# Attention's key and query loads issued by GpSimd, negated-maxima rows first in the sync engine's order, and a lead of 8 blocks in place of 12

## The reference

```python
x = x + attn(layernorm(x))      # 16 heads of 16; the part that the change touches
x = x + ffn(layernorm(x))       # ternary weights, squared relu, low-rank term
x = x + ssm(layernorm(x))       # scan over time, layernorm, gelu, projection
x = x + moe(layernorm(x))       # 16 experts, top 2

# attn: q, k, v = x @ Wq, x @ Wk, x @ Wv; heads of 16
attn = (einsum('bhqc,bhkc->bhqk', q1, k_eff1) + einsum('bhqc,bhkc->bhqk', q2, k_eff2)) * scale
attn = softmax(attn, axis=-1)
out  = einsum('bhqk,bhkd->bhqd', attn, v)      # then out @ Wo
```

## Time and profile before

| | |
|---|---|
| time, median of 3 runs | 1728.19 us |
| the profiled execution's own time | 1726.34 us |
| its span | 1724.6 us |
| PE / DVE / ACT / POOL busy | 88% / 68% / 57% / 25% |
| reductions L1912 | 512, 1221 ns each |
| exponentials L1950 | 1024, 599 ns each |

### The profile page before, as it was taken

One profiled execution on the slowest core, in us unless ns is written; L12 is line 12 of the kernel. 1 busy time (PEld: TensorE's weight loads), 2 busy tenths in 40 slices (PEclk: granted clock), 3 DMA queues, 4 the chain that ended last, 5 costly groups with the idle time before them and its releaser, 6 DMA issues. The chain is left out here.

```text
span 1724.6 us, 40236 instructions
## 1 busy us (share of the span) xinstructions
PE 1524.6 (88%) x14143; PEld 1004.6 (58%) x14144; DVE 1177.8 (68%) x2254; ACT 979.8 (57%) x2029; POOL 433.5 (25%) x682
## 2 busy tenths in 40 slices
PE   6999999999999999998699966999785499999990
PEld 5843333333333333336588865888673199999980
DVE  7688999999999999912578857554467822222225
ACT  3427888888888888880345512444222055555543
POOL 3055201101010101000112237222221045555540
PEclk9968999999999999997899976999896599999995
DMA  6950232333232323010100002333109432222218
GB/s 213 304 142 16 45 62 48 69 54 61 48 69 45 59 45 58 9 22 20 13 1 1 1 14 51 102 101 101 51 16 326 152 114 70 71 69 73 70 58 292
DMA packets 122967, 135.26 MB, mean 78 GB/s; under 512 B 29300, under 2 KB 93832, under 8 KB 122696
## 3 DMA queue, kind: packets, MB, share of 16 engines
q1 hardware_dynamic: 110056, 107.60, 24.3%
q0 software_dynamic: 7584, 20.72, 3.7%
q10 hardware_dynamic: 5184, 4.98, 0.8%
HBM read 92.23 MB, written 36.04 MB: 74 GB/s over the span
## 5 line engine op out<-in xcount | busy, mean ns | idle before, releaser
L1912 DVE TENSOR_REDUCE mx<-ps 128x1 f32<-128x1024 f32 x512 | 622.7, 1221 | 24.6 <-PE ps L2059 18.8
L1950 ACT ACTIVATE PR<-ps 128x512 f32<-128x512 f32 x1024 | 557.1, 599 | 87.4 <-PE ps L2113 37.5
L2059 PE MATMUL ps<-KQ 48*128 48x512 f32 x1024 | 389.1, 462 | 4.0 <-DVE mx L1912 3.6
L2113 PE MATMUL ps<-KQ 50*128 50x512 f32 x1024 | 379.9, 450 | 0.0
L2095 PE MATMUL ps<-PR,VO 128*32 128x256 f32 x4096 | 330.2, 394 | 9.1 <-ACT PR L1950 8.7
L2113 PEld LDWEIGHTS ps<-KQ 50*128 50x128 f32 x1024 | 155.2, 187 | 216.9 <-ACT PR L1950 199.6
L2095 PEld LDWEIGHTS ps<-PR,VO 128*32 128x32 f32 x4096 | 81.0, 108 | 196.0 <-ACT PR L1950 99.5
L2059 PEld LDWEIGHTS ps<-KQ 48*128 48x128 f32 x1024 | 158.9, 192 | 21.3 <-DVE mx L1912 20.6
L1804 PEld LDWEIGHTS ps<-e_xinT,e_w 128*128 128x128 f32 x1264 | 155.0, 194 | 5.8 <-issue 1.9
L1804 PE MATMUL ps<-e_xinT,e_w 128*128 128x128 f32 x1264 | 155.8, 277 | 1.1 <-ACT e_xinT L1736 1.1
L1794 PE MATMUL ps<-eW,e_hiddenT 128*128 x632 | 149.4, 380 | 0.0
(11 more groups left out here) (274 smaller groups left out, 2098.5 us busy)
## 6 DMA issues: line engine op xcount, KB each, us to landing
qk_parts<-parts SPq DMA_DIRECT2D x8, 2048.0 KB, 8.4
TB<-toeplitz_lines SPq DMA_DIRECT2D x32, 512.0 KB, 6.5
KQ<-qk_parts SPq DMA_DIRECT2D x96, 128.0 KB, 4.6
KQ<-qk_parts SPq DMA_DIRECT2D x192, 64.0 KB, 2.4
eW<-in_L_ffn_W SPq DMA_DIRECT2D x16, 512.0 KB, 6.9
eW<-in_L_ffn_W SPq DMA_DIRECT2D x8, 1024.0 KB, 13.2
e_got<-expert_outputs SPq DMA_DIRECT2D x16, 512.0 KB, 9.6
X<-in_L_attn_x SPq DMA_DIRECT2D x8, 512.0 KB, 4.4
```

What stands on the lines that cost most here:

```text
L1912: nc.vector.tensor_reduce(mx[:, u % RING, h * QT + q:h * QT + q + 1], ps[:, b:b + 2].rearrange("p a n -> p (a n)"), AX, ALU.max, negate=Tr ...
L1950: nc.scalar.activation(PR[:, kt % 2, h], ps[:, st_bank(u, s)], ACT.Exp).then_inc(exp_done, 1)
L2059: made = nc.tensor.matmul(ps[:, max_bank(u, t) + k], of_tile(queries(u % RING), h, q), kq[half(h, KROWS), 0, h % HR, k * BANK:(k + 1) * BA ...
L2113: nc.tensor.matmul(ps[:, st_bank(u, s)], kq[half(h, AROWS), 0, h % HR, kt * P:(kt + 1) * P], queries(u % RING)[half(h, AROWS), qc, h % HR] ...
```

## The change

Three things change.

1. `load_qk` takes the issuing engine and a semaphore. Units 0 and 1 are still loaded by SP during the projections; from unit 2 on GpSimd issues the DMAs (`load_half`) and counts them on `kq_late`. The 9 DMAs of a half follow a `negated_rows` of GpSimd: behind group (u, 1) the first half of unit u + 2, behind group (u, 0) the second half of unit u + 1.
2. SP's order within a unit is `rows(u, 1)`, then `heads(u - 1)`, then `rows(u + 1, 0)`; before it was `heads(u - 1)`, half a load, `rows(u, 1)`, half a load, `rows(u + 1, 0)`.
3. `LEAD` is 8 instead of 12, and `TURN` 1 instead of 2.

```diff
-    LEAD = 12
-    TURN = 2
+    LEAD = 8
+    TURN = 1
...
-                if u % 2 == 1 and u > 1 and t == 2 * LEAD:
+                if u % 2 == 1 and u > 1 and t == MAXES - QT:
                     invert_sums(dve, u // 2 - 1)
...
-        parts_stored(pool, 0)
+        for h in range(2):
+            parts_stored(pool, h)
...
+        def load_half(u, second):
+            pool.wait_ge(st_done, BLOCKS * (u - 2))
+            load_qk(pool, u, u % RING, range(second * LOADS // 2, (second + 1) * LOADS // 2), kq_late)
...
                 negated_rows(u, qc)
+                if u + qc < UNITS - 1 and u + qc > 0:
+                    load_half(u + qc + 1, 1 - qc)
                 if u < 2:
                     ffw.quantise(nc, pool, kept, QC * u + qc)
...
         rows(0, 0)
         for u in range(UNITS):
-            if u == 0:
-                sp.wait_ge(ones_ready, 2)
+            rows(u, 1)
             if u > 0:
                 heads(u - 1)
-            for some in (range(LOADS // 2), range(LOADS // 2, LOADS)):
-                if u + 2 < UNITS:
-                    sp.wait_ge(st_done, BLOCKS * u)
-                    load_qk(sp, u + 2, (u + 2) % RING, some)
-                if some.start == 0:
-                    rows(u, 1)
             if u + 1 < UNITS:
                 rows(u + 1, 0)
...
-            if t == 0:
-                pe.wait_ge(kq_loaded[u % RING], 16 * LOADS * (u // RING + 1))
+            if t == 0 and u < 2:
+                pe.wait_ge(kq_loaded[u], 16 * LOADS)
+            elif t == 0:
+                pe.wait_ge(kq_late[u % RING], 16 * LOADS * ((u - 2) // RING + 1))
```

More of the change, by code:

```diff
@@ L213, in transformer_kernel, with load_qk @@
                 QK_LOADS = K_LOADS + QC * 2 * len(PAIR_Q)
-                def load_qk(sp, u, r, some=range(QK_LOADS)):
+                kq_late = [sem(f"kq_late{r}") for r in range(RING)]
+                def load_qk(eng, u, r, some, loaded):
                     b, g = u // UPB, u % UPB
@@ L226, in load_qk @@
                             to, side, part, start, width = queries(r)[row:row + HD, qc], 0, PAIR_Q[j], BANK * qc, BANK
-                        sp.dma_start(to.bitcast(F32),
-                                     src[side, part, ds(g, 1), :, HR * y:HR * (y + 1), ds(SEQ * b + start, width)].rearrange("g c h t -> (g c) h t")).then_inc(kq_loaded[r], 16)
+                        eng.dma_start(to.bitcast(F32),
+                                     src[side, part, ds(g, 1), :, HR * y:HR * (y + 1), ds(SEQ * b + start, width)].rearrange("g c h t -> (g c) h t")).then_inc(loaded[r], 16)
                 with ExitStack() as s1:
@@ L270, in banks_free @@
                             eng.wait_ge(v_kept, NC + 1)
-                    att = attention(nc, sem, s2, sbuf, ps, KQ, queries, kq_loaded, load_qk, V, slot, sums, maxima, packed, heads_moved, weighed,
+                    att = attention(nc, sem, s2, sbuf, ps, KQ, queries, kq_loaded, kq_late, load_qk, V, slot, sums, maxima, packed, heads_moved, weighed,
                                     invert_sums, spread_inverses, weigh_heads, ffw, projected, parts_stored, banks_free)
@@ L293, in _ @@
                                         sp.wait_ge(stored[h2], 16 * 2)
-                                    load_qk(sp, u, u, range(second * QK_LOADS // 2, (second + 1) * QK_LOADS // 2))
+                                    load_qk(sp, u, u, range(second * QK_LOADS // 2, (second + 1) * QK_LOADS // 2), kq_loaded)
                             att.sync(sp)
@@ L1865, in _, with attention @@
                         nc.vector.tensor_tensor(chunk, chunk, flat(second[:, c % 2]), op=ALU.add).then_inc(added, 1)
-def attention(nc, sem, stack, sbuf, ps, KQ, queries, kq_loaded, load_qk, V, slot, sums, maxima, packed, heads_moved, weighed, invert_sums, spread_inverses, weigh_heads, ffw, projected, parts_stored, banks_free):
+def attention(nc, sem, stack, sbuf, ps, KQ, queries, kq_loaded, kq_late, load_qk, V, slot, sums, maxima, packed, heads_moved, weighed, invert_sums, spread_inverses, weigh_heads, ffw, projected, parts_stored, banks_free):
     kept = sums
```

## The result

The changed kernel takes 1896.71 us, median of 4 runs (1870.46 to 1905.07), against 1730.55 us for the kernel before (1727.22 to 1734.16, 4 runs). The forecast was 1812 us with a range up to 1870, so the direction was right and the size about half of what was measured: +166 us in place of +86. The ratio is 1.0875, 95% interval 1.0752 to 1.0998. The profiled execution took 1905.07 us, span 1903.4; it is the slowest of the four.

A forecast was written before the change was run, and what follows sets the result against it. TensorE was taken to pace attention's 1.23 us beat, with lost time not caught up. From 1726.3 us: -5 (start) + 40 (heads) + 1 (GpSimd) + 50 (clock) = +86, so 1812 us; range 1756 to 1870.

The forecast's parts named there:

- The start, -5 us: At attention's start, the first exponential comes at 120.4 us, 5.0 us earlier, and later attention moves as a whole.
- The heads behind the rows, +40 us: At the second group of units 1 to 15, the copy to OT starts 2.7 us late, 15 times.
- The rows: Before a group's copy to OT, rows land 1.9 us after issue, with 1.0 us spare for TensorE.
- GpSimd's own work, +1 us: In attention, idle time hides nine DMAs per group; late negated rows in units 0 and 1 cost 1 us.
- the lower end of 0.59: In GpSimd's queue, the low bound for one direct DMA, 0.59 us, taken from SP's row; 0.987 us was assumed.
- The rival with GpSimd as the bound: In attention, 2.8 us per GpSimd DMA makes a unit 55.3 us instead of 40.3; 1931 us, chance 0.07.
- The clock, +50 us: Behind the waits for heads, TensorE's clock falls 11 of 15 times at 4.5 us each; ends 0 and 90.
- The wait without falls (1762): In attention, the waits for heads come but the clock stays at 2.4 GHz; 1762 us, chance 0.14.
- The no-wait case: At the copy to OT, heads arrive in time and only the start's gain is left; 1720 us, chance 0.07.
- The forecast's upper end of 1870: At the copy to OT, heads 3.9 us late through contention with a fall every time; 1870 us.

The follow-up runs named there:

- experiment 4: The kernel before with LEAD 8, TURN 1 and the moved inversion, SP issuing rows, then heads, then the loads; 1874.97 us, ratio 1.0870.
- experiment 1: The changed kernel with the heads of the unit before sent ahead of the rows of the second group again; 1786.67 us, ratio 1.0399.
- 10: The changed kernel, LEAD still 8, with heads first, loads after the rows, and quantising of units 0 and 1 ahead of the load; 1728.83 us, ratio 0.9998.
- experiment 5: The changed kernel with LEAD 10 in place of 8; 1777.81 us, ratio 1.0175.
- 8: The kernel of 10 with the heads behind the rows in units 4, 8 and 12 alone; 1774.03 us, ratio 1.0257.
- experiment 3: The kernel before with LEAD 8, TURN 1 and the moved inversion, old orders on SP and GpSimd kept; 1741.80 us, ratio 1.0120.
- 9: The changed kernel with heads first, loads after the rows, quantising of units 0 and 1 ahead of the load, and LEAD 10; 1729.77 us, ratio 1.0013.
- experiment 7: The changed kernel with repeated matmuls keeping TensorE busy ahead of its two waits, second group of units 1 to 14; 1843.73 us, ratio 1.0643.

## Why the prediction was wrong, step by step

**The start, -5 us: right where it was placed, not at the end.** First exponential 120.4 forecast, 120.58 measured, and eight rows from 112.50 on made it in time. The forecast carried the 5 us to the end; in fact the clock rose 7.9 us later than before (150.4 against 142.5), which takes back some 5 us.

```profile
120.58 2.20 ACT L1952 ACTIVATE PR<-ps 128x512 f32<-128x512 f32 x4 [9.23 <-PE ps L2117]
```

**The heads behind the rows, +40 us: right.** Chain, distance and place hold. Where it stands alone (experiment 4) TensorE waits 2.9 us, against 2.7. In the changed kernel the copy's part is 18.0 us only, for the reason of the next point, but both waits together are 43.0.

**The rows: a term that was missing.** The forecast gave the rows the 1.9 us of an undisturbed landing and found 1.0 us spare. It did consider GpSimd's loads beside SP's DMAs, but only at the heads, and as an end of the range; the loads are issued with the rows, not with the heads. The rows had only that 1.0 us to spare, and full DMA engines cost them about 3 us more (5.1 from issue to use in place of 1.9). By itself it is worth 17.8 us of waiting and, with 5 falls, 58 us of time (experiment 1 against 10).

**GpSimd's own work, +1 us: right as far as can be seen.** No wait of TensorE behind 120 us goes back to it. Its DMA takes 508 ns, less than the lower end of 0.59. By the Trainium skill, page "SBUF — State Buffer", section "Who interferes with whom", `tensor_reduce` never contends for the port pair on trn2: the trace agrees, 508 ns on average and 4.53 us for nine beside a VectorE busy for 1.99 of 2 us. The 3.1 us that the same page of the Trainium skill, section "A bandwidth-pool intuition that's wrong (but worth ruling out)", gives for a DMA beside a `tensor_copy` do not appear. The rival with GpSimd as the bound falls with it.

**The clock, +50 us: the step that failed.** It had two factors, and both were too small. *How often:* 11 of 15 were to fall, 15 of 15 did. *How long:* a fall was priced at 4.5 us, between the 6.8 us stretch of the earlier trace rows and the 14 us of the earlier trace rows, which I took as the ends. Measured are 3.4 to 44.4 us, mean 21.5, that is 9.2 us a fall. 322 x 0.43 = 138 us in place of 50, some 18 of the 88 us by the number of falls (4 x 4.5) and 70 by their length: these 88 us are nearly all of the miss (span +178.8, forecast +86; what is left nets out of the start, the 6 us of the rest and the 9 us by which the sum in "Where the time went" is too high). The price of a slow microsecond, 0.43 us, was right; it carries the sums in the table. The error was to take two stretches for the bounds of a duration. The first was of another stage, and the second began well ahead of the first exponential: the earlier trace rows cut it at 128.5, and the record of the clock has it from 98.1 to 142.5 us, 44.4 us long (its first part in a thinner stage). That was the stretch to read, with the upper end at 0.43 x 44 = 19 us a fall and not 6.0. The trace before has 13 slow stretches in all, from 3.4 us to this one in a later and much thinner stage:

```profile
1323.60:1384.90 61.30, 27.08 (x93) 11.60 (x93) 49.92 (x245) 2.91 (x5) 5.04 (x5) 0.50 0.63 209
```

What decides how long the half clock stays is open: TensorE is busy nearly throughout, the same kind of wait is followed by 10 us once and 44 us another time, and single waits (experiments 1, 5 and 8) gave as long ones as fifteen in a row. The runs of the changed kernel differ by 35 us in the same way. Their mean granted clocks, 0.836, 0.839, 0.845 and 0.858, make 624, 611, 586 and 531 us at half clock over the whole span; at 0.43, the 93 us between the first and the last are 40 us, beside the 34.7 by which their spans differ. So the runs, too, differ by how long the clock stays low.

**The rivals.** The wait without falls (1762) has its mechanism in the profiled execution of experiment 3 alone, where waits of up to 1.5 us brought no fall; waits of the forecast's length always brought one. The no-wait case is experiments 9 and 10, and even its 1720 us was not reached. The forecast's upper end of 1870 had the falls right in number and not in length.

## What to carry to other kernels

Where TensorE's clock falls behind a wait, a periodic one of two to three microseconds cost the wait and two to three times as much again in the slow stretches behind it (44 and 0.43 x 259 = 111 us in experiment 4, 43 and 138 in the changed kernel); take as the upper end of that price the longest stretch that the trace shows, from its true beginning, and not a window cut out of it. A lead is cover for whole queues: before it is shortened, list all that lands in it, each with the traffic that will run beside it, since a transfer moved to another engine's queue loses the order that had kept it out of the way. What must land in a few microseconds goes first and bulk loads wait for its arrival; with that done, the lead of 8 cost nothing here, and it gained nothing either.

## What the runs showed of the hardware

- A wait of about 1 to 3 us of TensorE, between stretches at full load, can be enough for the clock to go from 1.00 to 0.50 (1.2 GHz): 15 of 15 in the changed kernel with 1.9 to 3.6 us per unit (2.9 on average, mostly in two pieces), 15 of 15 in experiment 4 with 2.2 to 3.8 us, 5 of 13 in experiment 1 with 1.4 us each on average, 3 of 10 in experiment 5 with 0.8, none of 6 in experiment 3 with 0.9. The slow stretches within attention lasted 3.4 to 44.4 us with TensorE busy again (26.83 of 27 us in one).
- The clock fell three times in experiment 7 with no wait of TensorE over 0.25 us, behind ten matmuls that ran one after another.
- A direct DMA issued by GpSimd takes 0.51 us of its time, beside VectorE's reductions.
- With the 16 DMA engines filled by loads of 64 and 128 KB, DMAs of 2 KB (rows) and of 4 and 64 KB (heads), issued in steps of 0.6 us, let their reader go on only 5.1 us and 6.8 us after the last of them was issued; undisturbed heads took 1.96 us.
- Two matmuls of 48 and 50 rows in different halves of the array run together (both at 197.73); in the same half they start 0.43 to 0.59 us apart, and the kernel takes 1.52 times as long, by estimate a little over half of it through a clock that never leaves 0.50 in attention.
